# Routed experts and the last attention of a transformer tower: weighting rows at evacuation, adding whole rows, and a later division

## The reference

```python
# layer 0, feed-forward: 16 experts, 4 per token; shared part for all tokens
y = sum_e w_full[:, e] * (silu(x @ Wu[e] + bu[e]) * (x @ Wg[e] + bg[e])) @ Wd[e] + w_full @ bd
y = y + (silu(x @ sWu + sbu) * (x @ sWg + sbg)) @ sWd + sbd
# layer 2, feed-forward: 8 experts, 2 per token, a shared part with its own weight
y = alpha * (silu(x @ ws_gate) * (x @ ws_up)) @ ws_down + (1 - alpha) * routed
# layer 3, attention: 12 heads of 16, keys mixed per head
attn = softmax((scores + content_bias) * SCALE)
out  = (attn @ v) @ Wproj.T + bproj
# layer 3, feed-forward: 8 experts, 2 per token, gelu(x @ w1[e]) @ w2[e], weighted and summed
```

## Time and profile before

| | us |
|---|---|
| Median of 3 runs | 3459.04 (3455.52 to 3487.1) |
| The profiled execution: its own time | 3445.02 |
| Its span, first to last instruction | 3443.3 |
| Mean granted TensorE clock | 0.782 |

### The profile page before, as it was taken

How to read it: one execution, slowest core, us unless ns; L and a number is a source line. 1 busy time by engine, 2 the same in 40 slices (tenths; PEclk the granted TensorE clock), 3 DMA queues, 4 the chain that set the end, 5 groups by cost and what they waited for, 6 DMA issues and landing times. The chain is left out here.

```text
span 3443.3 us, 35603 instructions
## 1 busy us (share of the span) xinstructions
PE 2611.6 (76%) x11340; PEld 1920.0 (56%) x11340; DVE 1738.9 (51%) x2602; ACT 1003.7 (29%) x2234; POOL 1000.2 (29%) x835
## 2 busy tenths in 40 slices
PE   7897079896677775777777655887898899982997
PEld 5555057674555553455555342776566666762776
DVE  2344324124999998499999854333223224432222
ACT  2202023104545553454555323222111112221211
POOL 0100475112543451255345111000314213313221
PEclk9786589657888988688898855675999876665999
DMA  9000123310000000000000000002103000013112
GB/s 204 9 0 32 68 79 109 89 40 1 0 1 0 0 0 0 0 1 1 0 0 0 1 19 9 1 0 64 38 27 94 10 1 0 1 30 120 41 35 64
DMA packets 86022, 102.29 MB, mean 30 GB/s; under 512 B 12025, under 2 KB 79496, under 8 KB 84933
## 3 DMA queue, kind: packets, MB, share of 16 engines
q1 hardware_dynamic: 71814, 75.18, 8.5%
q0 software_dynamic: 14080, 25.46, 2.2%
HBM read 57.77 MB, written 45.87 MB: 30 GB/s over the span
## 5 line engine op out<-in xcount | busy, mean ns | idle before, releaser
L1800 DVE TENSOR_TENSOR_SCAN mamba_f_state<-mamba_f_decay,mamba_f_inject 128x774 f32<-128x774 f32 x128 | 250.1, 1954 | 7.3 <-ACT mamba_f_decay L1696 6.5
L1800 DVE TENSOR_TENSOR_SCAN mamba_b_state<-mamba_b_decay,mamba_b_inject 128x774 f32<-128x774 f32 x128 | 250.0, 1953 | 7.4 <-ACT mamba_b_decay L1696 6.5
L1629 PE MATMUL mamba_b_y_ps<-mamba_b_seen,mamba_ident 128*128 128x258 f32 x768 | 218.6, 427 | 3.4 <-DVE mamba_b_seen L1807 2.8
L1629 PE MATMUL mamba_f_y_ps<-mamba_f_seen,mamba_ident 128*128 128x258 f32 x768 | 218.5, 426 | 3.4 <-DVE mamba_f_seen L1807 2.8
L1696 ACT ACTIVATE mamba_b_decay<-mamba_b_dt,mamba_b_A 128x256 f32<-128x256 f32 x384 | 164.8, 497 | 32.8 <-POOL mamba_b_dt L1552 26.5
L1696 ACT ACTIVATE mamba_f_decay<-mamba_f_dt,mamba_f_A 128x256 f32<-128x256 f32 x384 | 164.8, 497 | 32.8 <-POOL mamba_f_dt L1552 26.6
L1629 PEld LDWEIGHTS mamba_b_y_ps<-mamba_b_seen,mamba_ident 128*128 128x128 f32 x768 | 157.4, 219 | 29.3 <-DVE mamba_b_seen L1807 3.6
L1629 PEld LDWEIGHTS mamba_f_y_ps<-mamba_f_seen,mamba_ident 128*128 128x128 f32 x768 | 157.3, 219 | 29.3 <-DVE mamba_f_seen L1807 3.6
L2349 POOL TENSOR_TENSOR collab_keys<-collab_k_all,collab_mixing 108x1548 f32<-108x1548 f32 (+1 forms) x32 | 89.9, 2831 | 231.6 <-PE collab_s_ps L2606 146.0
L1602 PE MATMUL mamba_f_b_ps<-mamba_f_parts,mamba_sel 128*128 128x258 bf16 x128 | 40.0, 313 | 151.7 <-DVE mamba_f_seen L1807 151.0
L1602 PE MATMUL mamba_b_b_ps<-mamba_b_parts,mamba_sel 128*128 128x258 bf16 x128 | 40.0, 313 | 151.6 <-DVE mamba_b_seen L1807 150.9
(11 more groups left out here) (689 smaller groups left out, 6132.5 us busy)
## 6 DMA issues: line engine op xcount, KB each, us to landing
grouped_xs<-embed_empty SPq DMA_DIRECT2D x1, 7720.0 KB, 41.1
grouped_mlp_rows<-grouped_xs SPq DMA_DIRECT2D x20, 386.0 KB, 3.5
grouped_x_tok<-grouped_z SPq DMA_DIRECT2D x16, 384.0 KB, 5.9
geluexp_up<-in_geluexp_up SPq DMA_DIRECT2D x1, 4608.0 KB, 26.5
geluexp_down<-in_geluexp_down SPq DMA_DIRECT2D x1, 4608.0 KB, 37.4
shared_xs<-embed_empty SPq DMA_DIRECT2D x1, 3860.0 KB, 58.9
geluexp_xs<-embed_empty SPq DMA_DIRECT2D x1, 3860.0 KB, 43.0
shared_mlp_rows<-shared_xs SPq DMA_DIRECT2D x10, 386.0 KB, 3.4
```

Source lines behind the costliest of these rows:

```text
L1629: mm = pe.matmul(y_ps[:, c, 0:MT], ident[:], seen[:, n % 2, c, :], start=(n == 0), stop=(n == STATES - 1))
L1800: dve.tensor_tensor_scan(flat[0], flat[1], flat[2], 0.0, ALU.mult, ALU.add).then_inc(sem["scanned"], 1)
```

## The change

The weight of a choice travels with its row, as a further column (D + 1), from `pick`. VectorE multiplies a block's rows by it where it copied them before. `scale` is gone. In the summing, VectorE adds a group's rows, whole rows of 192 over up to four chunks, into `row_sum`; in grouped POOL adds choices 2 and 3 into `half_sum`. TensorE only turns the sums, two transposes per chunk, and VectorE adds them to h one group later. In shared the copy to `y` takes the shared part's weight along (four copies per group instead of one); in grouped the product of weights and biases moves into the dense part, with its own turning. Grouped's weights are loaded in another order and in one transfer more. In the attention `normalise` is split: `sum_up` after shift 1, the rest after shift 2; turning is in round 3, projection in round 0 of the item after, the addition to h after shift 3.

```diff
-ROW = D + 1
+ROW = D + 2
 route:
                 link(dve.tensor_reduce(pick[:, 0:k], chosen[:], AX.X, ALU.add))
+                link(dve.tensor_copy(x_tok[:, :, :, D + 1].rearrange("p c j -> p j c"), pick[:, 0:k]))
 shared_mlp, tensor (turn_weights: cn transposes of w_full to wt_ps; ScalarE copies them to wt):
+                        mm = pe.matmul(y_part(i, n), hid[:, q % 2, i * BLK:i * BLK + n], units[u]["down"],
+                                       start=(u == 0), stop=(w_full is None and u == U - 1))
+                        if w_full is not None and u == U - 1:
+                            if i == 0:
+                                pe.wait_ge(wt_ready, t + 1)
+                            mm = pe.matmul(y_part(i, n), wt[:, i * BLK:i * BLK + n], w_down, start=False, stop=True)
                     mm.then_inc(down_done, 1)
+                    if w_full is not None and u == U - 1 and t + 1 < NG:
+                        turn_weights(t + 1)
 shared_mlp, scalar, take(t):
-                    act.activation(y[0:n, c0:c0 + cn, :], y_ps[0:n, 0:cn, 0:D], ACT.Copy).then_inc(y_read, 1)
+                    for i in range(cn):
+                        ins = act.activation(y[0:n, c0 + i, :], y_part(i, n), ACT.Copy,
+                                             scale=1.0 if y_scale is None else y_scale[0:n, c0 + i:c0 + i + 1])
+                    ins.then_inc(y_read, 1)
 expert_blocks, gpsimd:
-                    if b < TC:
-                        pool.tensor_tensor(scale[:, b], ident[:].unsqueeze(1).broadcast_to([BLK, picks, BLK]),
-                                           pick[:, 0:picks, b:b + 1].broadcast_to([BLK, picks, BLK]),
-                                           ALU.mult).then_inc(scale_ready, 1)
+                if k == 4:
+                    for g, (c0, cn) in enumerate(TGROUPS):
+                        m = chunk_rows(c0)
+                        pool.wait_ge(z_loaded[g], 16 * k)
+                        if g >= 2:
+                            pool.wait_ge(row_sum_ready, g - 1)
+                        pool.tensor_tensor(half_sum[0:m, g % 2, 0:cn, :], x_tok[0:m, c0:c0 + cn, 2, 0:D],
+                                           x_tok[0:m, c0:c0 + cn, 3, 0:D], ALU.add).then_inc(half_ready, 1)
 expert_blocks, tensor:
-                        for i in range(2):
-                            for t, (lhs, rhs) in enumerate(terms):
-                                mm = pe.matmul(sum_ps[c % 2][:, i, 0:m], lhs[:, i * HALF:(i + 1) * HALF], rhs,
-                                               start=(t == 0), stop=(t == len(terms) - 1))
+                    pe.wait_ge(row_sum_ready, g + 1)
+                        for i in range(2):
+                            mm = pe.transpose(sum_ps[c % 2][:, i, 0:m], row_sum[0:m, g % 2, c - c0, i * HALF:(i + 1) * HALF],
+                                              ident[0:m, 0:m])
 expert_blocks, vector:
-                        dve.tensor_copy(y[:, (b - 2) % RING, :], y_ps[:, 0:D]).then_inc(y_ready, 1)
+                        dve.wait_ge(rows_loaded[q % 3], 16 * (q // 3 + 1))
+                        dve.tensor_scalar(sent_rows[:, (b - 2) % RING, :], y_ps[:, 0:D],
+                                          rows[:, q % 3, (b - 2) % FETCH, D + 1:D + 2], None,
+                                          ALU.mult).then_inc(y_ready, 1)
+                for g in range(NG):
+                    sum_rows(g)      # x_tok 0 + 1, + half_sum (grouped), + y (grouped, shared)
+                    if g:
+                        add_rows(g - 1)      # the additions to h
+                add_rows(NG - 1)
 grouped_experts, loads:
-                    (s_down[:], dram["grouped_s_down"]), (s_bias[:], dram["grouped_s_bias"]), (up[:], dram["grouped_up"]),
-                    (down[:], dram["grouped_down"]), (bd[:], dram["grouped_bd"])]
+                    (s_down[:], dram["grouped_s_down"]), (s_bias[:], dram["grouped_s_bias"]), (bd[:], dram["grouped_bd"]),
+                    (up[0:HALF], dram["grouped_up"][0:HALF]), (up[HALF:], dram["grouped_up"][HALF:]),
+                    (down[:], dram["grouped_down"])]
 attention, tensor:
-                    if i == 2 and b:
+                    if i == 3 and b:
                         turn_heads(b - 1)
-                    if i == 3 and b:
-                        project(b - 1)
+                    if i == 0 and b >= 2:
+                        project(b - 2)
 attention, scalar:
-                    if i == 2 and b:
+                    if i == 3 and b:
                         copy_heads(b - 1)
 attention, vector:
                     shift(r)
                     if i == 1 and b:
+                        sum_up(b - 1)        # class part and total, with a wait on att_ready
+                    if i == 2 and b:
                         normalise(b - 1)     # reciprocal and att
-                    if i == 0 and b >= 2:
+                    if i == 3 and b >= 2:
                         add_output(b - 2)
```

More of the change, by code:

```diff
@@ L961, in scatter_rows, with shared_mlp @@
                                     oob_is_err=False).then_inc(scattered, 16)
-def shared_mlp(nc, xn, name, units, bias, y, weights, scatter):
+def shared_mlp(nc, xn, name, units, bias, y, y_scale, w_full, w_down, ident, weights, scatter):
     U = len(units)
+    NG = len(TGROUPS)
     with Stage(nc, name + "_dense") as st:
@@ L999, in down @@
                     for i in range(cn):
-                        mm = pe.matmul(y_ps[0:n, i, 0:D], hid[:, q % 2, i * BLK:i * BLK + n], units[u]["down"],
-                                       start=(u == 0), stop=(u == U - 1))
+                        mm = pe.matmul(y_part(i, n), hid[:, q % 2, i * BLK:i * BLK + n], units[u]["down"],
[4 more added lines that the diff above has]
+                            mm = pe.matmul(y_part(i, n), wt[:, i * BLK:i * BLK + n], w_down, start=False, stop=True)
                     mm.then_inc(down_done, 1)
+                    if w_full is not None and u == U - 1 and t + 1 < NG:
+                        turn_weights(t + 1)
                 pe.wait_ge(loaded, count)
-                for t in range(len(TGROUPS)):
+                if w_full is not None:
+                    turn_weights(0)
+                for t in range(NG):
                     tokens, n = span(t)
@@ L1038, in _ @@
                         if u == 0 and t:
+                            if w_full is not None:
+                                take_weights(t)
                             take(t - 1)
-                take(len(TGROUPS) - 1)
+                take(NG - 1)
             @block.vector
@@ L1055, in _, with expert_blocks @@
                                                  in1=s[:, q % 2, 0:n], op0=ALU.add, op1=ALU.mult).then_inc(hid_ready, 1)
-def expert_blocks(nc, h, name, E, k, W, HID, pieces, act_fn, ones_row, up, down, weights, x_tok, pick, picks, home, xs,
-                  z, ident, scattered, scatter, y_shared, y_weight, w_full, w_down):
+def expert_blocks(nc, h, name, E, k, W, HID, pieces, act_fn, ones_row, up, down, weights, x_tok, home, xs, z, ident,
+                  scattered, scatter, y):
     NB = xs.shape[0] // BLK
@@ L1254, in _ @@
                         take_x(b + 2)
-                if w_full is not None:
-                    for c in range(TC):
-                        m = chunk_rows(c)
-                        act.wait_ge(wt_done, c + 1)
-                        act.activation(wt[:, chunk_cols(c)], xt_ps[0:w_full.shape[2], 0:m], ACT.Copy).then_inc(wt_ready, 1)
             @block.vector
```

116 lines of the change are left out of this document (76 added, 40 removed).

## The result

The changed kernel takes 3294.96 us (median of 4 runs, 3292.81 to 3301.48), the one before 3458.85 beside it: ratio 0.9505, 95% interval 0.9467 to 0.9544, 164 us. Forecast were 3262 us and a range of 3228 to 3350. The profiled execution of the changed kernel took 3292.81 us (span 3291.1), that of the kernel before 3445.02: 152 us less.

A forecast was written before the change was run, and what follows sets the result against it. No engine bounds the whole; TensorE bounds the grouped summing and, with stops and a low clock, the attention. Terms -79 - 7 - 4 - 4 + 0.6 - 98 = -191.4 from 3445.0 give 3254, with half of 14.0 3262 us; range 3228 to 3350.

The forecast's parts named there:

- rival A: Attention: clock does not follow, `att` waits for POOL's second product, TensorE still stands; 3345 us, chance 0.2.
- The summing: Three expert stages: VectorE adds whole rows, TensorE only turns sums; grouped -79, shared -7, GELU -4 us.
- its bound: Grouped summing: if POOL's half sum and VectorE never ran together, the end would be near 671, -71 us.
- The block loop: Expert blocks: weighted evacuation costs 0, POOL loses 17 scales between its sends; -4 us (0 to -10).
- The dense part: Grouped experts' dense part: weights come early, so its added work costs 0; +10 us if they come late.
- all this lies below the scatter: 0: Grouped dense part: with early weights, the added TensorE and ScalarE work is hidden by POOL's scatter, 0 us.
- The attention: Last attention: TensorE's stop of 1.92 us goes, 15 times; items take 10.2 us; -98 us.
- B: Attention: no stop, but TensorE's clock stays at the low level; +48 for -98, 3408 us, chance 0.1.
- C: Dense part: its added work shows, +10, 3272 us, chance 0.05.
- D: Slower: VectorE and POOL exclude each other more widely, evacuations and `att` wait; 3516 us, chance 0.03.

The follow-up runs named there:

- e5: The kernel before, unchanged, profiled a second time: 3465.75 us, ratio 1.0007.
- e1: The kernel before with only the new order of the attention stage: 3383.28 us, ratio 0.976.
- e3: The kernel before with routed rows one number longer and the copy of the weights into it, nothing else: 3458.77 us, ratio 0.9968.
- e13: The kernel before with only the shared rows' scatter spread over the dense part: 3441.09 us, ratio 0.997.
- e8: The changed kernel with the shared rows' scatter spread over the whole dense part, paced by VectorE's products: 3268.30 us, ratio 0.9452.
- e6: The changed kernel with TensorE's turn and projection and ScalarE's copy of the heads back in their old rounds: 3296.49 us.
- e7: The changed kernel with VectorE's sum, reciprocal and division back to back in one round, TensorE's turn and projection later: 3315.39 us.
- e12: e10 with the shared rows' scatter spread over half of the dense part, against the changed kernel's spread version e8: 3269.95 us.
- e10: e8 with the grouped rows' scatter held until the dense part's second product of five: 3268.43 us.

## Why the prediction was right, and where it was not

The time lies inside the range and 33 us above the forecast. That it lies inside is in part luck: the range reached up to 3350 for rival A, a low clock in the attention, which did not happen; the 47 us that were missed came from elsewhere. (Two sums are off by one: the terms of the grouped summing end near 662 and not 663, and 3254 with half of 14.0 is 3261 and not 3262. Nothing hangs on either.) By the steps of the prediction, first profile against the profile after:

- **The summing** was right in mechanism and size. Grouped: -79 forecast, -77.6 measured; from the last send to the last addition 32 us forecast, 34.2 measured. Shared: -7, measured -5.6. GELU: -4, measured -4.5. A row addition cost 0.958 (0.96), the first group had landed 9.9 us after the last send (8.5), and the exclusion of VectorE and POOL cost 1.44 us at each of the first two groups; after that VectorE had no wait for a half sum. That is near the value taken and not near its bound.
- **The block loop**: -4 forecast, -7.6 measured. TensorE's wait for rows is 4.2 us in two pieces instead of 12.2 in seven. The evacuation was mis-sized, 0.408 us in grouped (0.418 in the other two) for 0.348, inside its bounds and hidden.
- **The dense part**: the weights came early, as forecast: before, the loads still moved 27 GB/s from 345 to 376 us and ended near 442; now nothing is left to load after 345. It begins at 376.08, right after the routing. The step that failed is the one after it, "all this lies below the scatter: 0". In this profile the two stretches with dense parts are 47.3 us longer than in the first (20.4 and 26.9). But it did not fail by anything in the change: e5, e1 and e3 have these stalls with the old experts' code. What failed is the footing. The first profile showed an execution without late updates, at 3445, and the forecast carried that over to a run of the other kind. The 16 us between its span and e5's are +22.0 and +23.5 in the stretches with dense parts, -19.6 in the attention and -6.0 in the stage before it: large deviations that nearly cancelled. That the 14 us to the median came about in the same way is likely, since those runs took 3455 to 3487 us, where the kernel before lies on the chips with late updates (e13); but their profiles are not here.
- **The attention**: -98 forecast, -100.9 measured, items of 10.1 us (10.2), clock 0.96 (over 0.9), TensorE's waits for exponents 0.7 us (under 5). TensorE is what bounds it, as forecast: in 150 us from 2775 it is busy for 149.8. `att` was to fall between POOL's products or be 0.36 long; it lies in the first product and takes 0.8, with the end where the sum had it. The gain depends on the profile that it is held against: the old order took from 253.3 (e5) to 279.7 us (e13), the new one 172.0, so 81 to 108. What the prediction did not see is that either half of the edit would have given most of it.
- **Rivals.** A and B (the clock) did not happen, nor C: the weights were in time. D did not happen either: an evacuation takes 405 to 419 ns beside the sends, over 80 blocks.

With late updates on both sides the change is worth 168 us by the profiles (e5 to after, on different chips), and 164 by the runs beside each other. Without late updates an estimate is 152 + 47 = 199 us, near the forecast sum of 191; the changed kernel was not run on such a chip, so it stays an estimate.

Of the 14 us between the profiled execution and the median the forecast left in half. In the changed kernel the two kinds lie further apart, some 47 us by the stretches above: its attention took 168 to 172 us in every profile with both halves of the edit, so no shorter attention makes up for the late updates.

Open: why some executions keep pace with sixteen updates every 1.28 us and others don't, and what the late updates have to do with the queue of the transfers. Of the updates on record only TensorE's were late; what sets it apart from VectorE and ScalarE no run here shows. One candidate is the recording itself, since the updates' own records thin out where TensorE's come late, and no run here was without a recording of its cores' clock and span. The Trainium skill ("NOTIFIC — the notification-queue block", section "Overflow: three behaviours, one of which stalls the engine") has the block that writes such records hold back their producer when it is full inside, rather than lose a record there; no run here shows that it did, and here records are missing as well. Whether e8's spreading gains anything on a chip of the other kind was tried on the kernel before only (e13), where it gained nothing.

## What to carry to other kernels

Before adding up terms over one profile, see whether it is a usual one: a gap between the profiled execution and the median, even a small one, can be two large differences that cancel, and a second profile on another chip shows them. Where a wait ends "remote" on one chip's profile, compare the time of the semaphore's update with the end of the instruction that makes it, and count the updates of the indirect transfers beside it. A burst of indirect transfers from GpSimd that has slack is best spread under the work that hides it, paced by that work's own semaphore: a few lines gave some 26 us here, a sixth of what the whole change gave, and in e13, where it wasn't needed, it cost nothing that could be measured.

And where an engine stands once per item and its clock falls with it, find the work that it waits for and what stands in front of that. Here it was enough to move a division that nobody was waiting for out from in front of the shift that TensorE needed (e6), or to give TensorE a product of 1.09 us to do meanwhile (e7).

## What the runs showed of the hardware

- On some executions TensorE's semaphore updates come up to 69 us late (e12; 67 in e10) while GpSimd issues indirect transfers every 1.28 us. It begins with the work that ends 12 to 16 us after the first transfer (e10: scatter from 388.9, products that end at 401.3; changed kernel, shared: from 2356.8, products that end at 2372.4), and where updates are still held at the end of the scatter, they come within 10.5 us of its last transfer: in the changed kernel's shared experts the last transfer was issued at 2398.98, and four of TensorE's updates came between 2404.57 and 2404.78. At one transfer per 2.0 us (e12) or 3.7 us (e8) it does not occur beside the shared dense part.
- The records of the transfers' own updates thin out at the same time, 131 to 149 of 544 in the shared scatter. The timed runs move with the profiles (e8 27 us below the changed kernel, 25.0 by the profiles).
- A stop of TensorE of 1.02 us in each item of 11.3 (e7) left the granted clock at 1.00 for 150 us; stops of 1.92 in items of 17.2 went with a mean of 0.68 in the first profile. In e5 the kernel before, with stops of 1.76 to 1.94 in most items, had items from 12.3 to 19.1 and a mean of 0.74.
